# Halving the score steps of the last attention, and a new order of all steps, in a two-layer transformer kernel

## The chip, the cores and the metric

One Trainium2 chip; the program runs on one of its cores. The metric is device time in microseconds (us), the median of the runs shown. A core has a matrix engine (TensorE, PE in the rows; PEld is its weight load), a vector engine (VectorE, DVE), a scalar engine (ScalarE, ACT), GpSimd (POOL) and SyncE (SP), which here only issues transfers. Each engine works through its own list of instructions in order and waits on semaphores that the others raise.

## The reference, cut to what matters

Eight batch elements of 256 tokens by 128 features go through two transformer layers. Layer 0 has a sparse attention, with top-k selected keys, and a two-deep network of window attention and feed-forward parts. Layer 1 has a plain attention with 16 heads of size 8 and a mixture of 16 experts (8 chosen) and a shared one. The change touches only the attention of layer 1:

```python
qkv = x @ W_qkv.T + b_qkv                     # x: (8, 256, 128); 16 heads, head size 8
qkv = qkv.reshape(B, T, H, 3 * hs)
q = qkv[..., :hs]
k = qkv[..., hs:2 * hs]
v = qkv[..., 2 * hs:]
att = jnp.einsum('bthd,bshd->bhts', q, k) / math.sqrt(hs)
att_prob = jax.nn.softmax(att, axis=-1)
att_v = jnp.einsum('bhts,bshd->bthd', att_prob, v)
att_v = att_v.reshape(B, T, C)
return att_v @ W_out.T + b_out
```

All numbers are 32-bit floats.

## The kernel before

**Streams.** The eight batch elements are worked on in four rounds of two. Stream 0 (`s = 0`, memory `arena0`) takes one element of each round and stream 1 (`arena1`) the other; both run everything up to and with the last attention and the layer norm after it. A third stream runs the experts of all eight elements one after the other in the memory `late`. Every stream is a set of Python generators, one for each engine; a `yield` ends a step.

**What sets the order.** `STEPS_IN_TURN` has, for each engine, a string of pairs: a stream, and how many of its steps come next (base 36). So the order on each engine is written out in full, and an instruction can't pass one that stands ahead of it. `IN_ORDER` lists the semaphore signals that each kind of step raises. `BUSY` says how many small filler products (L591, `mean_mat`, results unused) TensorE does at each of 66 places in a round, while it would wait anyway. `LENT` says which bank the experts borrow for each of their results.

**Banks.** The accumulator memory `ps` has 8 banks of 128 rows by 512 floats; stream 0 owns banks 0 to 3 and stream 1 banks 4 to 7. `claim(banks, signals)` says with which signal a bank becomes empty again; in between the expert stream may borrow it.

**The last attention, for one element.** A head takes 16 of 128 rows, 8 of them its features and one a row for the maximum. There are two groups `G` of eight heads, and two halves of the 256 tokens, so four units `v`. In a unit:
- Scores (L1118): eight products. Product `(j, q)` uses rows 32q to 32q+31 and writes half `j` of bank `q`. A product of 32-bit floats is recorded as two MATMUL, so a unit is a row `x16` of the trace and an `x8` of the order.
- Maxima (L2049): VectorE reads banks 0 and 1 in one reduction and banks 2 and 3 in another, then writes the negated maxima (L2055) and raises `x_neg`. The scores of the next unit wait for that `x_neg`, since they write all four banks.
- After four units the maxima are turned (L1127) and added to the queries (L2062).
- Turned scores (L1157): for each unit the same eight products with queries and keys exchanged, again into all four banks. ScalarE takes one exponential for each bank (L1566), raises `st_exp` after each, and the next unit waits for the fourth.
- After units 1 and 3, `values1` (L1137) multiplies the probabilities with the values, into bank 0; ScalarE copies it out (L1260, `x_o`). Then come the sums (L1166), their reciprocal and the output product (L1172).

The stretches that the text calls scores, middle and experts' stretch of a round are: the scores of stream 0; the turned scores of stream 0 with the scores of stream 1; the turned scores of stream 1 with the experts of stream 0's element.

Of the kernel before, what the change touches and what calls it, by code (L numbers as in the profile page):

```python
# [49 lines left out]
def shape_constants():  # L50
# [47 lines left out]
    "pe": ("0912021302110213021204120e1206140317061707130213041305160313011401120212051302110213051308110c130a12011101120612"  # L98
            "02120613021a0317011a05150212021601120416051208110c12051105110216081106110213011202150218041c02150216011102180218"
            "0213021202130113011202110112011202120212041223012102210221021101261123122111210121112312211102211102112112021102"  # L100
            "2102110212031204110111021203210312032712211221021207120422022102210615011703130113012113022312231721160514041205"
            "120811071205110a110211081208120111021202190418031c041502150312021e0512031107120a12051402120811061102110112021702"
            "18041c041a011202180218021302120214011401110212011201120312011204112211012212220223022102110123112212011125112111"
            "0213210221022102112102122212211105120211032112022412031203122112031506172213221307132202210221072103190114011202"
            "22122113051304110512051103110c130a140211061402130617021301170215021a0612011801160112091308120c140a13021108110814"
            "01130217021a0415021502150112021802180213021202130113011202110112011202120112011204112211012212220223022102112202"
            "1123122302112102210221022111021121130521021102120312021301110323120326022512071221041202211202210722031201110112"
            "022117021321132113011902140414051305110312071105120111091102130814061102140115021f021a0415051a0416051208130c1105"
            "1107160811061102130112021502180317011502150217011802180213021202160212011101120312011202120212031122112712211124"
            "1124122111231121132n"),  # L110
# [231 lines left out]
def program(nc, A, out, idx_scratch, score_scratch):  # L342
    ctx = ExitStack()
    with ctx:
# [235 lines left out]
        def tensor_stream(pe, s):  # L580
# [265 lines left out]
            for r in range(ROUNDS):  # L846
# [295 lines left out]
                for v in range(4):  # L1142
                    G, c = v // 2, v % 2
                    if v == 2:
                        yield from values1(0)
                        yield
                        pe.wait_ge(*at("x_o", 1))
# [507 lines left out]
        def vector_stream(dve, st, s):  # L1655
# [147 lines left out]
            for r in range(ROUNDS):  # L1803
# [236 lines left out]
                for v in range(4):  # L2040
# [5 lines left out]
                    for half in range(2):  # L2046
# [3 lines left out]
                        if half == 0:  # L2050
                            yield
# [369 lines left out]
```

## Time and profile before

| | us |
|---|---|
| median of 3 runs | 1385.41 |
| the runs | 1385.41, 1389.0, 1380.8 |
| the profiled execution | 1387.57 |
| its span, first to last instruction | 1385.7 |
| TensorE busy | 1217.4 (88%) |
| VectorE busy | 906.4 (65%) |
| ScalarE busy | 878.2 (63%) |
| GpSimd busy | 364.9 (26%) |

The span is that of the trace; 1.9 us of the profiled execution lie outside it. "Busy" is the time in which at least one instruction ran on the engine, so products that run beside each other count once. TensorE is idle for 168 us, and part of its busy time is filler.

### The profile page before, as it was taken

What the parts mean: (1) busy time and instruction counts of PE and PEld (TensorE: products, weight loads), DVE (VectorE), ACT (ScalarE), POOL (GpSimd) and SP (SyncE); (2) the same over time, 40 slices, a digit from 0 to 9 for tenths busy, and PEclk for the clock granted to TensorE, in tenths of its full rate; (3) what the DMA queues carried; (4) which work ended last, traced back from release to release, by engine and by line L of the source; (5) the groups of instructions that cost most, each with busy time, mean ns of one, the idle gap of its engine ahead of it and who ended that gap; (6) DMA issues with size and microseconds to landing.
All of it is one profiled execution on the core that took longest, in us unless ns stands there. A gap on an engine that the chain in (4) does not pass through costs nothing.

```text
span 1385.7 us, 29670 instructions
## 1 busy us (share of the span) xinstructions
PE 1217.4 (88%) x11271; PEld 847.7 (61%) x11271; DVE 906.4 (65%) x2920; ACT 878.2 (63%) x2243; POOL 364.9 (26%) x580
## 2 busy tenths in 40 slices
PE   7779988789999898888899988887998989889897
PEld 6446655556676665555667755554676656556566
DVE  3966577657475867665766677765667486666533
ACT  3426687646665777755865777764847556874573
POOL 0710232212340423310532143311324042321022
PEclk9889999999999999999999999999999988999998
DMA  8121000000120000000112000000021000000000
GB/s 304 47 79 28 2 1 1 1 5 1 55 75 21 15 2 1 1 1 5 50 24 84 4 6 1 1 1 5 2 74 56 19 17 2 1 0 1 1 1 9
DMA packets 31791, 34.82 MB, mean 25 GB/s; under 512 B 19169, under 2 KB 23713, under 8 KB 31137
## 3 DMA queue, kind: packets, MB, share of 16 engines
q1 hardware_dynamic: 31648, 32.92, 7.9%
q8 instruction: 90, 1.47, 0.4%
q14 instruction: 53, 0.43, 0.1%
HBM read 25.46 MB, written 7.44 MB: 24 GB/s over the span
## 4 chain that ended last, share of the span: by engine, by line
PE 52%; DVE 20%; ACT 18%; issue 4%; DMA 1%; SPq 1%; POOL 1%; DVEq 0%; POOLq 0%; ACTq 0%
PE ps L624 4%; ACT arena L1513 4%; PE ps L1222 3%; ACT arena L1260 3%; DVE small L2049 3%; PE ps L804 3%; PE ps L1232 2%; PE ps L1213 2%; PE ps L687 2%; ACT arena L1566 2%; PE ps L1044 2%; PE ps L746 2%; PE ps L731 2%; PE ps L1118 2%; PE ps L762 2%
## 5 line engine op out<-in xcount | busy, mean ns | idle before, releaser
L1260 ACT ACTIVATE arena<-ps 128x512 f32<-128x512 f32 (+5 forms) x544 | 255.3, 490 | 203.9 <-PE ps L770 29.3
L2231 POOL TENSOR_TENSOR arena<-arena 128x512 f32<-128x512 f32 x64 | 81.9, 1289 | 262.0 <-DVE arena L1722 260.7
L1513 ACT ACTIVATE arena<-arena,small 128x128 f32<-128x128 f32 (+1 forms) x256 | 130.2, 513 | 7.4 <-DVE small L1986 7.2
L1697 DVE CUSTOM_DVE_ANT_0 arena<-ps,mask_w_bf 128x128 f32<-128x128 f32 (+1 forms) x256 | 67.6, 320 | 83.1 <-PE ps L746 82.9
L2049 DVE TENSOR_REDUCE small<-ps 128x4 f32<-128x1024 f32 x64 | 75.4, 1219 | 29.1 <-PE ps L1118 28.8
L1910 DVE TENSOR_TENSOR gath<-ps,rank_tab 96x512 f32<-96x512 f32 x96 | 62.3, 681 | 34.5 <-PE ps L632 22.6
L1566 ACT ACTIVATE arena<-ps 128x512 f32<-128x512 f32 x128 | 66.5, 607 | 26.8 <-PE ps L1157 26.7
L1222 PE MATMUL ps<-w_experts,late 128*128 128x128 f32 x544 | 72.8, 288 | 7.2 <-DVE late L2157 6.7
L1222 PEld LDWEIGHTS ps<-w_experts,late 128*128 128x128 f32 x544 | 68.5, 200 | 15.6 <-DVE late L2157 9.5
L1460 ACT ACTIVATE arena<-arena,small 128x224 f32<-128x224 f32 (+1 forms) x128 | 56.8, 448 | 27.3 <-DVE small L1934 27.1
L2101 DVE SCALAR_TENSOR_TENSOR late<-ps,late 128x128 f32<-128x128 f32 x128 | 39.3, 354 | 52.7 <-PE ps L1222 51.4
L804 PE MATMUL ps<-w_wqkv,arena 128*128 128x512 f32 x128 | 64.2, 637 | 10.4 <-DVE arena L1675 7.7
L1685 DVE TENSOR_TENSOR arena<-arena,small 128x512 f32<-128x512 f32 x96 | 69.9, 728 | 3.1
L591 PE MATMUL ps<-mean_mat 128*128 128x256 bf16 x437 | 62.9, 286 | 9.0 <-ACT arena L1260 4.3
L687 PE MATMUL ps<-packed,arena 128*128 128x128 f32 x384 | 63.2, 289 | 6.6 <-DVE arena L1688 3.6
L1213 PE MATMUL ps<-late,w_experts 128*128 128x256 f32 x256 | 67.2, 401 | 1.8 <-ACT arena L1260 1.7
L1232 PE MATMUL ps<-late,w_experts 128*128 128x256 f32 x256 | 66.8, 395 | 0.8 <-ACT arena L1260 0.7
L687 PEld LDWEIGHTS ps<-packed,arena 128*128 128x128 f32 x384 | 44.6, 146 | 28.9 <-issue 23.9
L2324 POOL TENSOR_TENSOR late<-late 128x256 f32<-128x256 f32 x32 | 23.6, 739 | 145.2 <-ACT late L1634 143.3
L624 PE MATMUL ps<-hot_ring,arena 128*96 128x512 bf16 x192 | 51.3, 407 | 11.6 <-DVE gath L1910 5.7
L591 PEld LDWEIGHTS ps<-mean_mat 128*128 128x128 bf16 x437 | 42.5, 102 | 28.2 <-issue 13.9
L1213 PEld LDWEIGHTS ps<-late,w_experts 128*128 128x128 f32 x256 | 49.4, 199 | 14.0 <-ACT arena L1260 3.6
(296 smaller groups left out, 2980.5 us busy)
## 6 DMA issues: line engine op xcount, KB each, us to landing
idxb<-idx_scratch SPq DMA_DIRECT2D x24, 512.0 KB, 5.2
score_scratch<-arena SPq DMA_DIRECT2D x96, 64.0 KB, 1.7
w_experts<-in_experts SPq DMA_DIRECT2D x3, 1088.0 KB, 16.2
w_wqkv<-in_wqkv SPq DMA_DIRECT2D x1, 1536.0 KB, 9.3
arena<-score_scratch SPq DMA_DIRECT2D x96, 16.0 KB, 2.0
arena<-in_x SPq DMA_DIRECT2D x8, 128.0 KB, 2.1
out_x<-late SPq DMA_DIRECT2D x8, 128.0 KB, 1.9
packed<-in_packed SPq DMA_DIRECT2D x2, 503.0 KB, 4.1
```

The lines of the kernel that those rows point to most:

```text
L591: mm(to, still[:, 0:P], still, start=True, stop=True)
L624: last = mm(bank[g % 2][0:GF, :], m.kv_part[i][:, 0, :], hot[n][:, part], start=(i == 0), stop=(n < 2 and i == 2))
L687: last = pe.transpose(bank[2][:, cols(h)], probs[:, h, :], ident[:, :])
L804: mm(bank[2 * k + j], m.sh[:, cols(k)], wqkv[:, l, 512 * j:512 * j + 512], start=True, stop=True)\
L1213: last = mm(bank[:, L * h:L * h + L], experts[:, 0, 4 * i - 3 + 2 * j + h, :], late.hT, start=True, stop=True)
L1222: last = mm(ups[j][:, L * h + P * k:L * h + P * k + P], late.moe_h[:, first:first + P], experts[:, 2, e, :], start=True, stop=True)
L1232: last = mm(ups[j][:, L * h:L * h + L], experts[:, 1, 4 * i - 3 + 2 * j + h, :], late.hT, start=True, stop=True)
L1260: return act.activation(dst, src, ACT.Copy)
L1513: ins = act.activation(probs, probs, ACT.Exp, bias=nb[s][:, i, h:h + 1], scale=cqs[s][:, T, hh_:hh_ + 1], accum_out=ls[s][:, i, h:h + 1])
L1566: act.activation(m.PT1[v][:, q, :, :].rearrange("p j n -> p (j n)"), bank[q], ACT.Exp, scale=SCALE_1)\
L2049: st.mark(dve.tensor_reduce(to, src, AX.X, ALU.max))
L2231: ins = pool.tensor_tensor(own, own, turned, ALU.add)
```

## The change

The four banks of a unit are handled as two halves: banks 0 and 1 (half 0) and banks 2 and 3 (half 1). A half has four products instead of eight. In the scores, VectorE signals each of its two reductions (`x_max`), and a half waits only for the reduction that read its two banks. In the turned scores, a half waits for the two exponentials that read its banks. For unit 2, half 1 is issued ahead of the value product of units 0 and 1, and half 0 (which shares bank 0 with it) behind; for unit 3, half 1 comes first too. The instructions on VectorE and ScalarE are the same, one to one, but for when they wait; ScalarE has 86 loads of its function tables in place of 88. TensorE has 494 filler products in place of 437. The strings of steps, fillers and banks lent are new from end to end, for all engines.

```diff
 STEPS_IN_TURN = {
-    "pe": ("0912021302110213021204120e1206140317061707130213041305160313011401120212051302110213051308110c130a12011101120612"
+    "pe": ("0912021102120212021204120712071209120812051202120211071203120112011102120213011302130216021305180816071105120511"
...
-    "last_mm": ["x_proj"] * 3 + ["x_mm"] * 4 + ["m_turned"] + ["st_mm"] * 2 + ["x_pv"] + ["st_mm"] * 2 + ["x_pv", "x_sum", "x_out"],
-    "last_act": ["x_q", "x_v"] + ["st_exp"] * 8 + ["x_o"] + ["st_exp"] * 8 + ["x_o", "x_rs"],
-    "last_dve": ["x_k"] + ["x_neg"] * 4 + ["x_aug", "x_on"],
+    "last_mm": ["x_proj"] * 3 + ["x_mm"] * 8 + ["m_turned"] + ["st_mm"] * 5 + ["x_pv"] + ["st_mm"] * 3 + ["x_pv", "x_sum", "x_out"],
+    "last_act": ["x_q", "x_v"] + ["st_exp"] * 10 + ["x_o"] + ["st_exp"] * 6 + ["x_o", "x_rs"],
+    "last_dve": ["x_k"] + ["x_max", "x_max", "x_neg"] * 4 + ["x_aug", "x_on"],
...
-                    claim(range(4), ("x_neg", v + 1))
...
-                        pe.wait_ge(*at("x_neg", v))
-                    pe.wait_ge(*at("x_own", G + 1))
-                    for j in range(2):
-                        for q in range(4):
...
+                    for half in range(2):
+                        yield
+                        claim([2 * half, 2 * half + 1], ("x_max", 2 * v + half + 1))
...
+                        if v > 0:
+                            pe.wait_ge(*at("x_max", 2 * v + half - 1))
+                        if half == 0:
+                            pe.wait_ge(*at("x_own", G + 1))
+                        for j in range(2):
+                            for q in (2 * half, 2 * half + 1):
...
+                def turned_scores(v, half):
                     G, c = v // 2, v % 2
+                    yield
+                    claim([2 * half, 2 * half + 1], ("st_exp", 4 * v + 2 + 2 * (half if v < 2 else 1 - half)))
+                    if v == 0:
+                        if half == 0:
+                            keep_busy(bank[1][:, 0:L])
+                            pe.wait_ge(*at("x_aug", 1))
+                    elif (v, half) == (2, 0):
                         pe.wait_ge(*at("x_o", 1))
+                    elif v == 3:
+                        pe.wait_ge(*at("st_exp", 4 * v - 2 * half))
                     else:
-                        pe.wait_ge(*at("st_exp", 4 * v))
+                        pe.wait_ge(*at("st_exp", 4 * v - 2 + 2 * half))
                     for j in range(2):
-                        for q in range(4):
+                        for q in (2 * half, 2 * half + 1):
...
+                for v in range(2):
+                    for half in range(2):
+                        yield from turned_scores(v, half)
+                yield from turned_scores(2, 1)
+                yield from values1(0)
+                yield from turned_scores(2, 0)
+                for half in (1, 0):
+                    yield from turned_scores(3, half)
                 yield from values1(1)
```

**Place 1: TensorE, scores of stream 0 in the last round.** L1118 (L1119 after) are the scores of stream 0; L1060, L1068 and L1079 (L1059, L1067, L1078 after) are the feed-forward products of stream 1. Before:

```order
L1118 MATMUL ps<-arena0 128x256 x8
L1060 MATMUL ps<-arena1,w_w1 128x256 x2
L1060 MATMUL ps<-arena1,w_w1 85x256
L1068 MATMUL ps<-arena1,w_w1 128x256 x2
L1068 MATMUL ps<-arena1,w_w1 85x256
L1118 MATMUL ps<-arena0 128x256 x8
L1079 MATMUL ps<-arena1,w_w2 128x256 x3
```

After:

```order
L1119 MATMUL ps<-arena0 128x256 x8
L1059 MATMUL ps<-arena1,w_w1 128x256 x2
L1059 MATMUL ps<-arena1,w_w1 85x256
L1119 MATMUL ps<-arena0 128x256 x8
L1067 MATMUL ps<-arena1,w_w1 128x256 x2
L1067 MATMUL ps<-arena1,w_w1 85x256
L1119 MATMUL ps<-arena0 128x256 x8
L1078 MATMUL ps<-arena1,w_w2 128x256 x3
L1119 MATMUL ps<-arena0 128x256 x4
```

Three pairs of halves and the first half of the last unit stand among the feed-forward products of stream 1, where two of the four units stood.

**Place 2: TensorE, the middle of the last round.** L1157 (L1159 after) are the turned scores of stream 0, L1118 (L1119) the scores of stream 1, L1137 the value product. Before:

```order
L1157 MATMUL ps<-arena0 128x256 x8
L1118 MATMUL ps<-arena1 128x256 x8
L1137 MATMUL ps<-arena0 32x256 x16
L1157 MATMUL ps<-arena0 128x256 x8
L1118 MATMUL ps<-arena1 128x256 x8
L1157 MATMUL ps<-arena0 128x256 x8
L1118 MATMUL ps<-arena1 128x256 x8
L1137 MATMUL ps<-arena0 32x256 x16
L1118 MATMUL ps<-arena1 128x256 x8
```

After:

```order
L1159 MATMUL ps<-arena0 128x256 x8
L1119 MATMUL ps<-arena1 128x256 x8
L1159 MATMUL ps<-arena0 128x256 x8
L1119 MATMUL ps<-arena1 128x256 x8
L1159 MATMUL ps<-arena0 128x256 x4
L1137 MATMUL ps<-arena0 32x256 x16
L1119 MATMUL ps<-arena1 128x256 x4
L1159 MATMUL ps<-arena0 128x256 x8
L1119 MATMUL ps<-arena1 128x256 x8
L1159 MATMUL ps<-arena0 128x256 x4
L1119 MATMUL ps<-arena1 128x256 x4
L1137 MATMUL ps<-arena0 32x256 x16
```

The same work stands in ten runs of scores in place of eight (one of the eight stands ahead of the rows shown), four of them single halves, and one half stands ahead of the first value product.

**Place 3: ScalarE, the last round, where the exponentials of stream 1 meet the experts.** L1566 (L1575 after) are the exponentials, L1611 and L1620 (L1617, L1626) the SiLU of the experts, ACT_TABLE_LOAD a load of a function table, L1634 (L1640) the weighting of two experts. Before:

```order
L1566 ACTIVATE arena1<-ps 128x512 x4
L1600 ACTIVATE late<-ps 128x32
L1604 ACTIVATE late<-ps 128x256
L1605 ACTIVATE late<-ps 128x128
L1251 ACT_TABLE_LOAD
L1611 ACTIVATE late<-ps 128x256
L1620 ACTIVATE late<-ps 128x512 x2
L1249 ACT_TABLE_LOAD
L1566 ACTIVATE arena1<-ps 128x512 x4
L1251 ACT_TABLE_LOAD
L1620 ACTIVATE late<-ps 128x512 x2
L1260 ACTIVATE arena1<-ps 128x256
```

After:

```order
L1575 ACTIVATE arena1<-ps 128x512 x6
L1275 ACTIVATE arena0<-ps 128x256
L1575 ACTIVATE arena1<-ps 128x512 x2
L1281 ACTIVATE arena0<-ps,eps_col 128x256
L1285 ACTIVATE arena0<-arena0 128x256
L1575 ACTIVATE arena1<-ps 128x512 x2
L1270 ACTIVATE arena1<-ps 128x256
L1606 ACTIVATE late<-ps 128x32
```

Ten of the sixteen exponentials stand ahead of the experts' first instruction where four stood; fewer changes of table are left behind it.

## Rows read from the trace of the kernel before

**Rows 1.** The page: the span, and each engine's busy time with its instructions.

```profile
span 1385.7 us, 29670 instructions
...
PE 1217.4 (88%) x11271; PEld 847.7 (61%) x11271; DVE 906.4 (65%) x2920; ACT 878.2 (63%) x2243; POOL 364.9 (26%) x580
```

**Rows 2.** The page: the chain that ended last, by engine.

```profile
PE 52%; DVE 20%; ACT 18%; issue 4%; DMA 1%; SPq 1%; POOL 1%; DVEq 0%; POOLq 0%; ACTq 0%
```

**Rows 3.** Groups by line: count | busy us, mean ns | idle before, releasers.

```profile
L2049 DVE TENSOR_REDUCE small<-ps 128x4 f32<-128x1024 f32 x64 | 75.4, 1219 | 29.1 <-PE ps L1118 28.8
...
L1566 ACT ACTIVATE arena<-ps 128x512 f32<-128x512 f32 x128 | 66.5, 607 | 26.8 <-PE ps L1157 26.7
...
L591 PE MATMUL ps<-mean_mat 128*128 128x256 bf16 x437 | 62.9, 286 | 9.0 <-ACT arena L1260 4.3 <-ACT arena L1341 3.6 <-DVE arena L1707 1.0
...
L1251 ACT ACT_TABLE_LOAD x43 | 55.2, 1283 | 0.8
...
L1118 PE MATMUL ps<-arena 32*128 32x256 f32 x512 | 38.0, 412 | 13.2 <-DVE arena L2055 11.5 <-POOL arena L2305 1.7
L1157 PE MATMUL ps<-arena 32*128 32x256 f32 x512 | 37.4, 406 | 7.4 <-ACT arena L1566 5.7 <-DVE arena L2062 1.0 <-ACT arena L1260 0.5
```

**Rows 4.** Windows, the four score stretches summed: all work, then L591 alone.

```profile
sum 66.00, PE 55.86 PEld 38.20 DVE 52.54 ACT 19.30 POOL 6.43; mean PE 13.96 PEld 9.55 DVE 13.13 ACT 4.83 POOL 1.61
...
sum 66.00, PE 3.88 PEld 2.73; mean PE 0.97 PEld 0.68
```

**Rows 5.** Windows, the four middle stretches summed: all work, then L591 alone.

```profile
sum 119.00, PE 95.77 PEld 61.15 DVE 67.52 ACT 58.57 POOL 12.92; mean PE 23.94 PEld 15.29 DVE 16.88 ACT 14.64 POOL 3.23
...
sum 119.00, PE 9.17 PEld 6.96; mean PE 2.29 PEld 1.74
```

**Rows 6.** Windows, the four experts' stretches summed: all work.

```profile
sum 161.00, PE 148.16 PEld 106.83 DVE 91.38 ACT 128.25 POOL 41.51; mean PE 37.04 PEld 26.71 DVE 22.84 ACT 32.06 POOL 10.38
```

**Rows 7.** Timeline, TensorE, scores of the last round: start us, us, what.

```profile
1263.59 1.15 PE L1118 MATMUL ps<-arena 32*128 32x256 f32 x16
...
1266.40 1.99 PE L1044 MATMUL ps<-arena,w_wo 128*128 128x256 f32 x8 [0.48 <-ACT arena L1260]
1268.32 1.15 PE L1118 MATMUL ps<-arena 32*128 32x256 f32 x16
...
1270.72 0.70 PE L605 MATMUL ps<-arena,mean_mat 128*128 128x256 f32 x2
1272.15 1.15 PE L1118 MATMUL ps<-arena 32*128 32x256 f32 x16 [0.73 <-DVE arena L2055]
1273.23 1.56 PE L1060 MATMUL ps<-arena,w_w 128*128 128x256 f32 x6
```

**Rows 8.** Chain of waits, third round and (last row) last round: start us, us, what.

```profile
954.64 2.08 ACT arena L1566 x4
...
956.76 1.93 PE ps L1137 x32
...
962.33 0.19 DVE arena L2055
...
962.56 1.19 PE ps L1118 x16
...
963.77 2.37 DVE small L2049 x2
...
1302.76 2.35 DVE small L2049 x2
```

**Rows 9.** Timeline, TensorE, middle of the last round.

```profile
1283.44 1.15 PE L1157 MATMUL ps<-arena 32*128 32x256 f32 x16 [1.02 <-DVE arena L2062]
1284.87 1.99 PE L1098 MATMUL ps<-arena,packed 128*128 128x256 f32 x8 [0.29 <-DVE arena L1668]
...
1293.01 1.15 PE L1157 MATMUL ps<-arena 32*128 32x256 f32 x16 [0.51 <-ACT arena L1260]
1293.98 1.04 PE L1118 MATMUL ps<-arena 32*128 32x256 f32 x16
```

More of the change, by code:

```diff
@@ L1105, in tensor_stream @@
                     G, T = v // 2, v % 2
[L1106 to L1121 removed]
+                    for half in range(2):
+                        yield
+                        claim([2 * half, 2 * half + 1], ("x_max", 2 * v + half + 1))
+                        if (v, half) == (0, 0):
+                            keep_busy(bank[1][:, 0:L])
+                            pe.wait_ge(*at("x_k", 1))
+                            pe.wait_ge(*at("x_v", 1))
+                        if v > 0:
[4 more added lines that the diff above has]
+                            for q in (2 * half, 2 * half + 1):
+                                rows_ = slice(32 * q, 32 * q + 32)
+                                last = mm(bank[q][:, L * j:L * j + L], m.q_own[rows_, G, j, cols(T)], m.k1[rows_, G, :],
+                                          start=True, stop=True)
+                        last.then_inc(*one("x_mm"))
                 yield
@@ L2042, in vector_stream @@
                     yield
+                    for half in range(2):
+                        if half == 1:
+                            yield
+                        dve.wait_ge(*at("x_mm", 2 * v + half + 1))
+                        src = ps[:, 4 * s + 2 * half:4 * s + 2 * half + 2, :].rearrange("p q (j n) -> p q j n", j=2)
+                        to = mx1[s][:, T, 8 * G + 4 * half:8 * G + 4 * half + 4].rearrange("p (q j) -> p q j", j=2)
+                        dve.tensor_reduce(to, src, AX.X, ALU.max).then_inc(*one("x_max"))
+                    yield
                     if v == 0:
                         dve.wait_ge(*at("m_zero", 1))
-                    dve.wait_ge(*at("x_mm", v + 1))
-                    for half in range(2):
-                        src = ps[:, 4 * s + 2 * half:4 * s + 2 * half + 2, :].rearrange("p q (j n) -> p q j n", j=2)
-                        to = mx1[s][:, T, 8 * G + 4 * half:8 * G + 4 * half + 4].rearrange("p (q j) -> p q j", j=2)
-                        st.mark(dve.tensor_reduce(to, src, AX.X, ALU.max))
-                        if half == 0:
-                            yield
-                    yield
-                    st.wait()
+                    dve.wait_ge(*at("x_max", 2 * v + 2))
                     to = m.mneg[:, T, G, :].rearrange("p (h n) -> p h n", n=HR)[:, :, D1]
```

120 lines of the change are left out of this document (48 added, 72 removed).

## The prediction, made before the change was run

> **What bounds the kernel now.** I read the page first. TensorE is busy 88% of the span, the next engine 65% [rows 1], and the chain of waits lies on TensorE for 52% and on VectorE and ScalarE for 38% [rows 2]. So no engine is the bound by itself: TensorE has 168 us of idle time, and where the chain leaves it, something short and serial is under way. Then I looked at the stretches that the change touches. Score and middle stretches together last 185 us; in them TensorE idles 10.1 + 23.2 us and spends 3.9 + 9.2 us on fillers, 46.4 us in all [rows 4, 5]. The experts' stretches, 161 us, have only 12.8 us idle, so TensorE is 92% busy there [rows 6]. The reader is to see two regimes: a middle in which waits for banks set the pace, and a stretch behind it in which TensorE's own work does.
>
> In the middle the wait is a ping-pong between an engine and the banks. For scores: reductions 2.37, negation 0.19, products 1.19, and the little time between, a period of 3.83 (the second L1118 of the pattern runs from 962.56, its reductions from 963.77; 962.33 is the negation before it) [rows 8]. For turned scores: exponentials 2.08 and products 1.19, about 3.33. VectorE has 64 reductions of 1219 ns and ScalarE 128 exponentials of 607 [rows 3], and neither overlaps with the products of its own stream.
>
> **What a half costs TensorE.** This decides the case. A full unit is eight products in four row tiles, two to a tile. One product over the full array, of the same 256 columns, takes 0.70 us, and four take 1.99, so 0.43 more for each. Eight in four tiles take 1.15, which is what two in a row should take (0.70 + 0.43 = 1.13) [rows 7]. So the tiles run beside each other, and the time goes by the products in one tile. A half has four products in two tiles: again two to a tile. My value is that it lasts 1.15 and keeps the engine 1.08, the time from a unit's start to that of the next product of full size (1272.15 to 1273.23) [rows 7]. It does half the work in the time of the whole, since two tiles stand idle. The other end is half the price, 0.54, if the products were limited by how fast they are issued; the 0.43 per product speaks against that. A half that stands right behind the other half, with its wait already over, uses the idle tiles, so such a pair costs one unit. The trace of before has no such pair; I take the tiles as independent because the four of a unit are.
>
> In the new order the 128 halves stand in 85 runs where 64 units stood: 45 single halves, 37 pairs, 3 triples. At least 21 more run times: 21 × 1.08 = 23 us. If no pair overlapped, because its second half still waits, 64 × 1.08 = 69 us.
>
> There is a rule against the change beside this. A unit of row tiles followed by another of row tiles starts it 0.97 later (1293.01 to 1293.98) [rows 9], a product of full size 1.08 later [rows 7]: a change of tiling costs some 0.1. With 21 more runs and a change at either side that is 42 × 0.11 = 4.6 us at most, and it is already in the 1.08. The Trainium skill, TensorEngine Tiling (Array Packing), section Key Properties, says that a change of tiling mode drains TensorE; it gives no price. The trace agrees in sign with its 0.11, and by the rule the sum would be no other.
>
> **The change part by part.**
>
> *Score stretches.* Alone, with halves, VectorE never waits: while it reduces one half, the other is refilled, 1.15 for 1.18. The period falls from 3.83 to 2.37 + 0.19 = 2.56, for three transitions 3.8 us per element. But stream 1's feed-forward lies between. In the last round the stretch takes 1263.59 to 1283.44, 19.9 us [rows 7, 9]. Following the new order (pair, L1059, pair, L1067, pair, L1078, two halves) with the durations above, L1059 (1.56 [rows 7]) and its like ahead of a waiting half and two extra VectorE steps of the feed-forward between, I come to about 16.6. Saved 3.2 at best; I take 2, since each wait met late passes to both streams.
>
> *Middle stretches.* The last round, from the first turned score (t = 0). Unit 0 of stream 0 gives exponentials from 1.2 to 3.3; its unit 1 follows in halves at 2.25 and 3.3, exponentials until 5.6. Half (2,1) must wait for all of unit 1, since its banks come free last: 5.6, exponentials 6.8 to 7.8. The value product (1.93 [rows 8]) runs behind it, 6.4 to 8.3, its copy to 8.8, then (2,0) and (3,1), exponentials 10.0 to 12.1, and (3,0), until 13.3. Stream 1's scores stand between: reductions 2.2 to 4.5, 4.8 to 7.1, then its (2,0), which is held behind the value product until 8.3: 9.5 to 12.1, and 12.3 to 14.7. Before, the same ran from 1283.44 to 1305.11 (1302.76 + 2.35), 21.7 us, of which 2.0 are L1098, now ahead [rows 8, 9]: 19.7. Saved 5.0 on paper, if all is in time. The stretch would hold 8 units' work in 10 runs and at least two pairs whose second half waits. I take 3.5.
>
> *Experts' stretches.* Stream 1's turned scores are 8 halves for 4 units. In the last round 6 runs, elsewhere similar: 2.2 us more if all pairs overlap, 4.3 if none does. TensorE is 92% busy, so it is paid; I take 3. The shorter wait of ScalarE gains nothing there, since the experts filled it.
>
> *Table loads.* 88 to 86; the two that go stand in the last round, where the exponentials of stream 1 go ahead of the experts (place 3). ScalarE is on the chain there, 1.28 each [rows 3]: −2.6. The other end is 0.
>
> *Fillers.* 57 more of 62.9/437 = 0.144 us [rows 3]: 8.2 us if none was covered. 36 of the 57 stand in the first eight places of the two streams, while weights load; the rest where a wait is due. I take +1; below nothing is possible too, if they keep the clock up.
>
> *All other steps.* They are the same instructions in a new order, over the 1040 us outside the stretches, with 168 − 10.1 − 23.2 − 12.8 = 122 us of TensorE idle [rows 1, 4 to 6]. I see no term in it and take 0, with ±8 (some 2 us a round either way, the size of one wait moved).
>
> Sum: 4 × (−2 − 3.5 + 3) − 2.6 + 1 = −11.6. On the profiled execution, 1387.6, that is 1376.0; that execution lies 2.2 above the median of the runs shown, 1385.4, so the same on the median is 1373.8. I predict 1375.
>
> **The rivals.**
>
> *A, the chain gives all of it (faster still).* Pairs overlap whenever they stand together, and the walks above come true: 4 × (−3.2 − 5.0 + 2.2) − 2.6 = −26.6, about 1359. For it: 33.3 us of plain idle in the two kinds of stretch. Against: stream 1's halves are held behind stream 0's waits on one in-order engine. Chance 0.20.
>
> *B, given back (no change).* Stream 1 gets its scores sooner but its turned scores meet the dense experts' stretch, and TensorE pays 4.3 there, 2 more in the scores and middle each: 4 × (−5.5 + 4 + 4.3) would be +11; with half of the extra work in time that was idle, about 0: 1386. For it: 92%. Chance 0.25.
>
> *C, TensorE becomes the bound (slower).* No half overlaps another: 69 us of new TensorE time. It decides once this exceeds what the stretches have to give: 46.4 idle and filler, of which some 16 can't be used, since dense windows too keep 8% idle. So 69 − 30 = 39 more, less the 22 of waits saved: +17, 1402. For it: half (1,1) waits for a reduction 1.18 behind that of (1,0), longer than the 1.08 the first keeps the engine. Against: where feed-forward products stand ahead of the pair, both waits are over. Chance 0.15.
>
> *D, the new order outside loses (slower).* A transfer or an expert's bank comes due later; +8 on no gain, 1394. Nothing in the profile speaks for it but the size of the move. Chance 0.07.
>
> My forecast has 0.33, its own range 1366 to 1384. That the change does nothing at all is excluded by the order.
>
> **How the numbers follow.** Within 0.5% (about 7 us) of 1385.4 is what a measurement can't tell from no change: 1378.5 to 1392.3. Faster: A 0.20, the forecast 0.28, B 0.04: 0.52. Same: the forecast 0.05, B 0.19, D 0.02: 0.26. Slower: C 0.15, D 0.05, B 0.02: 0.22. The range 1355 to 1396 leaves out most of C and the lower edge of A, some 0.2.
>
> **What would show it.** L1119 should be recorded in runs of 8 that last 1.15, not 0.6, and TensorE's busy time should rise by 15 to 45 us. Of a pair that wasn't waiting, all 16 records should fit in 1.15 to 1.4. VectorE's idle time before its reductions (29.1) and ScalarE's before the exponentials (26.8) [rows 3] should fall by half. The middle of the last round should take 15 to 17 us. I am wrong if a half lasts 0.6 (then A or better), if TensorE's idle time outside the stretches has moved by more than 10, or if the experts' stretches grew by more than 5 each.

## The result, and the profile after

The changed kernel takes 1395.41 us (median of 17 runs, 1386.25 to 1401.99) against 1384.25 us (17 runs, 1375.12 to 1389.34) for the kernel before in the same comparison: 1.0082 of it, 95% interval 1.0064 to 1.0099. It is 0.8% slower; 1375, faster, had been predicted, in a range of 1355 to 1396 whose upper end belonged to the rivals. Three executions of other kernels (two with the third stretch new, one with the pairs put together), more than 1.5% above the fastest of their kernel at a lower clock, are left out of the ratios and means below. The page of the profiled execution, answering to [rows 1] and, in its last line, to [rows 2]:

```profile
span 1393.2 us, 29754 instructions
...
PE 1240.4 (89%) x11328; PEld 867.4 (62%) x11328; DVE 901.7 (65%) x2920; ACT 877.4 (63%) x2241; POOL 365.8 (26%) x580
...
PE 51%; ACT 18%; DVE 17%; issue 4%; POOL 3%; DMA 2%; SPq 1%; POOLq 0%; DVEq 0%; ACTq 0%
```

TensorE is busy 23.0 us more and idle 15.5 us less (152.8 for 168.3), and the span grew by 7.5. GpSimd and the transfers hold more of the chain than they did. The groups that answer to [rows 3]:

```profile
L2055 DVE TENSOR_REDUCE small<-ps 128x4 f32<-128x1024 f32 x64 | 76.8, 1220 | 19.2 <-PE ps L1119 19.1
...
L1575 ACT ACTIVATE arena<-ps 128x512 f32<-128x512 f32 x128 | 67.6, 599 | 23.6 <-PE ps L1159 23.6
...
L590 PE MATMUL ps<-mean_mat 128*128 128x256 bf16 x494 | 77.6, 289 | 5.4 <-ACT arena L1351 2.4 <-ACT arena L1270 1.8 <-DVE arena L1713 1.2
...
L1119 PE MATMUL ps<-arena 32*128 32x256 f32 x512 | 56.4, 398 | 6.5 <-DVE small L2055 4.5 <-POOL arena L2311 1.1 <-issue 0.7
L1159 PE MATMUL ps<-arena 32*128 32x256 f32 x512 | 54.7, 399 | 5.7 <-ACT arena L1575 3.0 <-DVE arena L2068 1.6 <-ACT late L1626 0.2
```

The idle time before the reductions fell from 29.1 to 19.2 and that before the exponentials from 26.8 to 23.6. The two groups of scores take 111.1 us of TensorE for 75.4, the fillers (the small products with unused results) 77.6 for 62.9. The timeline of TensorE over the last round's scores and the beginning of its middle (start us, us, what), beside [rows 7, 9]:

```profile
1278.27 1.16 PE L1119 MATMUL ps<-arena 32*128 32x256 f32 x16 [0.30 <-POOL arena L2311]
1279.39 1.56 PE L1059 MATMUL ps<-arena,w_w 128*128 128x256 f32 x6
1280.88 2.09 PE L1119 MATMUL ps<-arena 32*128 32x256 f32 x16
1282.91 1.56 PE L1067 MATMUL ps<-arena,w_w 128*128 128x256 f32 x6
1284.40 1.21 PE L1119 MATMUL ps<-arena 32*128 32x256 f32 x16
1285.54 1.56 PE L1078 MATMUL ps<-arena,w_w 128*128 128x256 f32 x6
1287.03 1.13 PE L1119 MATMUL ps<-arena 32*128 32x256 f32 x8
...
1296.10 1.16 PE L1159 MATMUL ps<-arena 32*128 32x256 f32 x16
1297.07 1.15 PE L1119 MATMUL ps<-arena 32*128 32x256 f32 x16
...
1301.72 1.13 PE L1159 MATMUL ps<-arena 32*128 32x256 f32 x8
1302.78 1.93 PE L1137 MATMUL ps<-arena 128*32 128x256 f32 x32
...
1312.72 1.13 PE L1176 MATMUL ps<-arena,packed 128*128 128x512 f32 x2
```

A single half (`x8`) lasts 1.13 and the two halves of an unwaiting pair together (`x16`) 1.16; where the second half waits, the pair lasts up to 2.09. The scores of this round go from 1278.27 to 1296.10, 17.8 us (19.9 before), and the middle to the sums at 1312.72, 16.6 us. Before, the sums came 19.2 us after the first turned score, but 2.0 of these were stream 1's L1098, whose counterpart L1097 now stands in the scores' stretch.

So the place that was changed did get shorter. Where the time went shows in windows over everything else, from the end of stream 1's last attention to the beginning of stream 0's next (and from the start of the program to the first): first all work, then the fillers alone; of the kernel before,

```profile
sum 982.00, PE 871.69 PEld 601.66 DVE 668.27 ACT 645.78 POOL 288.82; mean PE 217.92 PEld 150.42 DVE 167.07 ACT 161.44 POOL 72.21
...
sum 982.00, PE 46.62 PEld 30.46; mean PE 11.66 PEld 7.61
```

and of the one after:

```profile
686.00:934.00 248.00, 221.84 (x2130) 154.09 (x2128) 168.64 (x571) 171.21 (x461) 81.33 (x130) 0.97 0.08 23
1012.00:1275.00 263.00, 234.51 (x2216) 165.00 (x2216) 172.45 (x579) 179.76 (x474) 85.99 (x136) 0.95 0.08 23
sum 1013.50, PE 895.14 PEld 622.91 DVE 677.95 ACT 663.72 POOL 308.26; mean PE 223.79 PEld 155.73 DVE 169.49 ACT 165.93 POOL 77.07
...
sum 1013.50, PE 65.93 PEld 41.07; mean PE 16.48 PEld 10.27
```

Outside the last attentions the kernel is 31.5 us longer: 19.3 of fillers, 8.1 of idle time (118.4 for 110.3) and 4.1 of other TensorE work. The last attentions are 24.0 us shorter (403.7 to 379.7). The difference, 7.5, is the span's.

Not all of the 24.0 is a gain, and not all of the 31.5 a loss: work has moved from the one to the other. The same windows hold 17.9 us more of ScalarE's work (645.78 to 663.72) and 19.4 more of GpSimd's (288.82 to 308.26), while the whole kernel has no more of either (878.2 and 877.4, 364.9 and 365.8). The fillers in them are 421 for 313, of 57 more in all. What the halves alone are worth is read from the first experiment.

### The profile page after: what moved, and what is told of

Its sections match the earlier page's. It is cut to its first block, busy times and chain, and to the rows that moved or that the text cites. A ratio compares the mean times of both kernels' runs of the same rounds, so it can differ in the third digit from the quotient of the medians.

```text
span 1393.2 us, 29754 instructions
## 1 busy us (share of the span) xinstructions
PE 1240.4 (89%) x11328; PEld 867.4 (62%) x11328; DVE 901.7 (65%) x2920; ACT 877.4 (63%) x2241; POOL 365.8 (26%) x580
## 4 chain that ended last, share of the span: by engine, by line
PE 51%; ACT 18%; DVE 17%; issue 4%; POOL 3%; DMA 2%; SPq 1%; POOLq 0%; DVEq 0%; ACTq 0%
ACT arena L1523 4%; ACT arena L1270 4%; PE ps L623 3%; PE ps L1159 3%; PE ps L1232 3%; PE ps L1119 3%; PE ps L803 3%; PE ps L1223 3%; PE ps L1242 2%; PE ps L1137 2%; PE ps L686 2%; DVE arena L1703 2%; DMA idxb<-idx_scratch 2%; PE ps L745 2%; ACT arena L1575 2%
## 5 line engine op out<-in xcount | busy, mean ns | idle before, releaser
L1270 ACT ACTIVATE arena<-ps 128x512 f32<-128x512 f32 (+6 forms) x544 | 254.9, 489 | 213.3 <-PE ps L769 30.4
L2055 DVE TENSOR_REDUCE small<-ps 128x4 f32<-128x1024 f32 x64 | 76.8, 1220 | 19.2 <-PE ps L1119 19.1
L1575 ACT ACTIVATE arena<-ps 128x512 f32<-128x512 f32 x128 | 67.6, 599 | 23.6 <-PE ps L1159 23.6
L590 PE MATMUL ps<-mean_mat 128*128 128x256 bf16 x494 | 77.6, 289 | 5.4 <-ACT arena L1351 2.4
L1916 DVE TENSOR_TENSOR gath<-ps,rank_tab 96x512 f32<-96x512 f32 x96 | 62.5, 681 | 27.7 <-PE ps L623 13.7
L686 PE MATMUL ps<-packed,arena 128*128 128x128 f32 x384 | 62.3, 286 | 15.3 <-DVE arena L1698 4.8
L590 PEld LDWEIGHTS ps<-mean_mat 128*128 128x128 bf16 x494 | 47.6, 103 | 30.9 <-issue 17.6
L2163 DVE TENSOR_TENSOR late<-late,ps 128x512 f32<-128x512 f32 x64 | 43.3, 684 | 32.4 <-PE ps L1242 27.3
L803 PE MATMUL ps<-w_wqkv,arena 128*128 128x512 f32 x128 | 61.4, 614 | 1.7 <-DVE arena L1681 1.6
L1119 PE MATMUL ps<-arena 32*128 32x256 f32 x512 | 56.4, 398 | 6.5 <-DVE small L2055 4.5
L745 PE MATMUL ps<-arena 64*128 64x192 f32 (+1 forms) x512 | 56.9, 345 | 5.4 <-DVE small L1992 3.9
```

Of the source, the lines that this page charges most:

```text
L590: mm(to, still[:, 0:P], still, start=True, stop=True)
L686: last = pe.transpose(bank[2][:, cols(h)], probs[:, h, :], ident[:, :])
L745: last = mm(bank[j][:, n * i:n * i + n], m.qT[rows_, 2 * half + i, cols(T)], m.kT[rows_, 2 * half + i, key_cols(T)], start=True, stop=True)
L803: mm(bank[2 * k + j], m.sh[:, cols(k)], wqkv[:, l, 512 * j:512 * j + 512], start=True, stop=True)\
L1119: last = mm(bank[q][:, L * j:L * j + L], m.q_own[rows_, G, j, cols(T)], m.k1[rows_, G, :], start=True, stop=True)
L1270: return act.activation(dst, src, ACT.Copy)
```

## The experiments

All ratios are to the kernel before on the same chip, with 95% intervals. "Old order" is the kernel before with its own strings, fillers and lent banks; "in place" means that the two halves of a unit stand where the unit stood. The diffs are cut to the lines that matter.

**Halves alone, in the old order**

```diff
-                    claim(range(4), ("x_neg", v + 1))
+                    for half in range(2):
+                        claim([2 * half, 2 * half + 1], ("x_max", 2 * v + half + 1))
```

(The turned scores likewise. The strings stay; half (2,1) stays behind the value product.)

> The kernel before, with its strings of steps, its fillers and its lent banks untouched; only each unit of the last attention is written, waited for and freed in two halves, both halves in the step where the unit stood. Theory N (the new order outside the last attention costs, the halving gains): the halving keeps what the changed kernel's trace shows in the last attention, some 10 to 20 us, so 1365 to 1375 and a ratio of 0.987 to 0.993. Theory H (the halving itself costs, since a half keeps TensorE 1.13 us as a whole unit does, and other streams wait behind it): 1389 to 1397, ratio 1.003 to 1.009, as the changed kernel.

Measured 1373.79, ratio 0.9928 [0.9901, 0.9955]. Its groups of reductions and exponentials:

```profile
L2055 DVE TENSOR_REDUCE small<-ps 128x4 f32<-128x1024 f32 x64 | 75.3, 1216 | 17.7 <-PE ps L1120 17.6
...
L1572 ACT ACTIVATE arena<-ps 128x512 f32<-128x512 f32 x128 | 66.5, 606 | 19.2 <-PE ps L1161 19.1
```

Both waits shrink more than in the changed kernel (29.1 and 26.8 to 17.7 and 19.2). By the traces stream 0's time from its first scores to its sums, over the four rounds, fell from 160.6 to 152.1 us, which is about the gain. The halves are a gain of 0.7%; what turns it into a loss of 0.8% is the rest of the change.

**Scores alone, turned scores alone**

```diff
-                    claim(range(4), ("x_neg", v + 1))
+                        claim([2 * half, 2 * half + 1], ("x_max", 2 * v + half + 1))
```

in the first, and in the second only its counterpart:

```diff
-                    claim(range(4), ("st_exp", 4 * v + 4))
+                    claim([2 * half, 2 * half + 1], ("st_exp", 4 * v + 2 + 2 * half))
```

> As halves_in_old_order, but only the scores with the maxima (L1118, L2049) are halved; the turned scores stay whole. Theory N: VectorE's ping-pong is the longer one (3.83 against 2.56 us a unit), so over half of the gain of both, ratio 0.992 to 0.997. Theory H: in the scores most second halves must wait for a reduction and keep TensorE blocked, so this part carries the loss, ratio 1.002 to 1.006.

> As halves_in_old_order, but only the turned scores with the exponentials (L1157, L1566) are halved. Theory N: a quarter to a half of the gain of both, ratio 0.995 to 0.999. Theory H: half of its turned scores stand among the experts, where TensorE is 92% busy, so it loses there, ratio 1.001 to 1.005.

Measured 0.9948 [0.9931, 0.9965] and 1.0005 [0.9984, 1.0027]. The gain lies in the scores, whose banks VectorE reads. In the profiled executions the turned halves by themselves shorten the middle stretches by 1.8 us in all and lengthen the experts' stretches by 2.4; both are of the size by which these stretches differ from one kernel to another.

**The same instructions, but no early release**

```diff
+HALVED_X, HALVED_T = (), ()         # each half is signalled, the wait is for the whole unit
```

> The kernel before with the signals of the halves (x_max after each reduction, one signal for each half unit) but with every unit still issued whole and every wait for the whole unit, in the old order. If the 0.7% of halves_in_old_order come from the early release of the banks, this is the kernel before: 0.998 to 1.002. If they come from something beside it (other semaphores, code positions), it is as fast as halves_in_old_order, 0.991 to 0.996.

Measured 1.0013 [0.9982, 1.0044]; the reductions wait as before:

```profile
L2087 DVE TENSOR_REDUCE small<-ps 128x4 f32<-128x1024 f32 x64 | 75.4, 1218 | 28.2 <-PE ps L1121 27.9
```

28.2 stands against 17.7, and the gain is gone with it. It is the release by halves that gains, not the finer signals.

**Turned scores of one stream**

```diff
+HALVED_X, HALVED_T = (), (0,)       # the second run (1,)
```

> Old order; only the turned scores of stream 0, which stand in the middle stretches, are halved. The prediction's two regimes (gain where waits set the pace, loss where TensorE or ScalarE is dense) say: faster than halve_turned_only (1.0005), 0.996 to 0.999. If there are no such regimes: about half of nothing, 0.999 to 1.002.

> Old order; only the turned scores of stream 1, which stand among the experts, are halved. Two regimes: slower than the kernel before, 1.001 to 1.004. No regimes: 0.999 to 1.002.

Measured 1.0028 [1.0002, 1.0053] and 0.9984 [0.9963, 1.0005]. Both small, and in the direction opposite to what was expected: stream 1, among the dense experts, doesn't pay for its halves. The prediction's "two regimes" find no support here.

**One half ahead of the value product, in the old order**

```diff
+                        turned_half(2, 1)
                         values1(0)
-                        turned_half(2, 1)
                         turned_half(2, 0)
```

> halves_in_old_order, and half (2,1) of the turned scores moved ahead of the value product of units 0 and 1, with its two exponentials ahead of the copy out of bank 0, as the changed kernel has it; half 1 comes first in unit 3 too. The rest of the order is the old one. Theory N: the move is worth the 1 us for each element that two exponentials last, where ScalarE is waited for; 3 to 8 us under halves_in_old_order, ratio 0.987 to 0.991. Theory S: the lone half adds 1.08 us of TensorE each time, 8 in all, and eats it: 0.992 to 0.996.

Measured 0.9986 [0.9961, 1.0011], so 0.58% (8 us) slower than with both halves behind. ScalarE's copy of the value product now stands behind two more exponentials and the value product behind one more half (1.13), eight times in the kernel. The middle stretches, 76.5 us in all with both halves behind, are 82.9 with one ahead, and the experts' stretches 183.4 for 179.5; that the copy and the value product are the whole of it was not shown by itself.

**The new order with the old fillers; with the pairs put together**

```diff
-BUSY = [... of the changed kernel ...]
+BUSY = [... of the kernel before ...]
```

> The changed kernel with the table of fillers of the kernel before (437 small products, at the same 66 places of a round, in place of 494; their busy time grew from 62.9 to 77.6 us). Theory F (the fillers cost): it wins back 5 to 10 us, ratio to the kernel before 1.001 to 1.005. Theory N and H, in which the fillers run in idle time: within 3 us of the changed kernel, ratio 1.006 to 1.010.

```diff
+MERGED = {("x", 0, 0, 1): "E", ...}  # 24 of the 27 scattered pairs: both halves at one place
```

> The changed kernel, whose order leaves 27 pairs of halves of one unit apart (besides those of unit 2, which the value product parts). In 24 of them both halves now stand at one place, 23 at that of the first half and one at that of the second; every half still waits for its own banks alone, and nothing else moves. Theory S (the scattered halves cost: L1119 and L1159 keep TensorE busy 106.8 us here against 85.6 with the halves paired in the old order, and the difference is the loss): TensorE's score time falls by 10 to 20 us and the time by as much, so a ratio to the kernel before of 0.995 to 1.001. Theory N (the new order of everything else costs): the score time falls, the time stays within 4 us of the changed kernel, 1.005 to 1.011.

Measured 1.0307 [1.0279, 1.0334] and 1.0297 [1.0253, 1.034]. Neither mends anything. But the second run doesn't test what it was made for: the scores' time on TensorE was to fall by 10 to 20 us and is 108.5 for 106.8 (in the old order with all halves 85.6). In 23 of the 24 pairs the second half was drawn forward to the first, where it can hold up the queue until its banks are free. So it shows that joining the halves in this way costs 2% more; whether scattered halves cost something in the changed kernel stays open. In both kernels the mean granted clock of the profiled execution is 0.949, against 0.970 in the changed kernel:

```profile
core 0: 1430.9 us, clock 0.949
```

**No fillers at all: in the kernel before, and in the changed kernel**

```diff
-BUSY = [("b0h303...
+BUSY = [("000000...
```

> The kernel before without any filler product (L591, 437 of them, 62.9 us busy). new_order_old_fillers was 30 us slower than the changed kernel with fewer fillers at other places, and its granted clock fell from 0.97 to 0.949. Theory F (the fillers are worth what they keep up of TensorE's clock): the clock falls below 0.95 and the time rises by over 2%. The rival, that fillers are paid as work: the time falls.

> The changed kernel without any filler product. If its loss against the kernel before is one of the order, it is behind old_order_no_fillers by 0.5 to 2% as well. If the loss lies in its 57 additional fillers, or in where they stand, it is level with it or ahead.

Measured 1.0107 [1.0057, 1.0158] and 1.0212 [1.0171, 1.0252]. So all fillers together are worth 1.1% in the kernel before and 1.3% in the changed one: they don't cause the loss. Without any of them the changed kernel is still 1.04% slower, halves included.

**The two orders mixed.** Both orders pass through (nearly) the same state, the same number of steps taken by every stream on every engine, each time stream 0 begins a round. So the strings, fillers and lent banks can be cut there and joined. All of these kernels have the changed kernel's halves.

(The next two diffs are schematic: one word for each stretch or part, in place of the strings themselves.)

```diff
-STEPS_IN_TURN, BUSY, LENT = new, new, new, new
+STEPS_IN_TURN, BUSY, LENT = old, old, new, old   # third_round_new
```

> Both orders are cut at the three places where stream 0 begins a new round; there both have taken the same steps on every engine, but for 2 to 6. Each of the four stretches of steps, with its fillers and lent banks, can so come from the old order or from the new one. The halves are the changed kernel's everywhere. Old in all four is the old order with half (2,1) ahead, 0.9986 of the kernel before; new in all four is the changed kernel, 1.0082. Here the third stretch alone is new (old, old, new, old). Theory L, the loss lies in the stretch itself: in the traces the third round is 335.9 us long in the changed kernel and 325.0 in the old order with the half ahead, so +10.9 us or 0.8%: 1.006, and the round is 333 to 338 long. Rival W, the loss is spread or is handed on from earlier stretches: a quarter of 0.96%, 1.001. Rival J, orders that were made whole lose wherever they are joined: 1.008 or more.

> The counterpart: new, new, old, new. Theory L: the changed kernel less 10.9 us, 1.0082 - 0.0079 = 1.000, the third round 323 to 327 us long. Rival W: 1.0082 - 0.0024 = 1.006. Rival J: 1.01 or more.

> Old, new, old, new. By the starts of stream 0's rounds in the traces the new order loses 5.7 us in the first stretch, gains nothing or 0.5 in the second, loses 10.9 in the third and gains 0.4 in the fourth. Theory L: level with the old order throughout, 0.998 to 0.999. Rival W: half of the loss, 1.003. Rival J: 1.01 or more.

> Old, new, new, new. Theory L: the changed kernel less the 5.7 us of the first stretch, 1.004, with the third round still 333 to 338 us long. Rival W: 1.006; the two are near each other here, and the length of the first round tells (312 against 317 us for the start of stream 0's second round). Rival J: 1.01.

| stretches | ratio | third round of stream 0, us |
|---|---|---|
| old old old old (the half ahead; not cut) | 0.9986 [0.9961, 1.0011] | 324.9 |
| old old **new** old | 1.0085 [1.0052, 1.0117] | 334.8 |
| new new old new | 1.0124 [1.0090, 1.0158] | 331.9 |
| old new old new | 1.0158 [1.0121, 1.0195] | 328.4 |
| old new new new | 1.0160 [1.0115, 1.0205] | 334.9 |
| new new new new (the changed kernel; not cut) | 1.0082 [1.0064, 1.0099] | 335.8 |

With the third stretch alone new the kernel is as slow as the changed one, and the round has the length that theory L gave it (333 to 338). But L had 1.006 for the kernel and J 1.008 or more, so the ratio of 1.0085 fits J better. The converse fails: taking the third stretch out again, or the first, makes the kernel slower still, as rival J had it. One reason shows at the joins. In the changed kernel stream 0's first products of the round (L855) stand ahead of stream 1's last scores (L1119),

```profile
645.43 0.38 PE L855 MATMUL ps<-packed,arena 128*128 128x128 f32 x2
645.74 1.16 PE L1119 MATMUL ps<-arena 32*128 32x256 f32 x16
```

and in third_round_old the cut has put them (L813 there) behind (L1077, L1085):

```profile
642.63 1.38 PE L1077 MATMUL ps<-arena 32*128 32x256 f32 x16
645.82 1.13 PE L1077 MATMUL ps<-arena 32*128 32x256 f32 x8 [1.81 <-DVE small L2013]
648.49 1.11 PE L1085 MATMUL ps<-packed,arena 128*128 128x128 f32 x4 [1.54 <-DVE arena L2019]
649.40 0.64 PE L813 MATMUL ps<-packed,arena 128*128 128x128 f32 x2
```

From stream 0's sums to its next round it is 15.3 us there and 8.4 in the changed kernel: three or four steps, moved by the cut, come with 7 us. It is the cut and not the change of order that does this: in first_round_old both sides of this join are new, and it is 13.1 us. The join in third_round_new moved nothing of this (7.6 us, as in the old order), so it is the cleaner one; the one at the end of its third stretch is 9.5 for 7.9. No run cuts the old order and joins it again unchanged, so how much of these ratios the joins cost is not known.

Where the round gets longer the traces tell without any join, in the changed kernel itself (each is one execution). In microseconds of stream 0's third round:

| kernel | start to first scores | first scores to sums | sums to next round |
|---|---|---|---|
| old order, half ahead | 276.2 | 40.9 | 7.9 |
| changed kernel | 291.8 | 35.5 | 8.5 |
| third stretch new | 289.9 | 35.5 | 9.5 |

Stream 0 loses 13.7 to 15.6 us on its way to the last attention and wins 5.4 back in it. Over all four rounds of the changed kernel it is 28.2 us lost on the way and 13.2 won in the attentions. So the loss lies outside the last attention, and over half of it in the third round. It can be placed more closely by the output products of stream 0's two window layers. From the first to the second it is 56.2, 64.7, 56.5 and 60.4 us in the four rounds of the old order with the half ahead, and 66.6, 61.7, 74.7 and 67.1 in the changed kernel; with the third stretch alone new it is 73.1 in that round. This distance takes up the whole loss.

**Inside the third stretch.** Both orders meet twice more in it: in stream 0's gather, and in its second window layer.

```diff
-third stretch = new, new, new
+third stretch = old, old, new     # third_round_last_part_new; the other has old, new, new
```

> Within the third stretch both orders pass through the same state twice more, with no step moved by a cut there: in stream 0's gather (some 60 us into the round) and in its second window layer, once its first queries and keys are turned (some 225 us in). Here only the part behind the second cut is new, until the next round begins; all else is old with the half ahead (0.9986; with the whole third stretch new 1.0085). In the trace of the latter stream 0 has its second f_o 14.9 us later in the round than in the old order, its first 1.7 earlier, stream 1 its first 7.6 later. Theory E, the delay is made ahead of the cut and handed down: 1.000 at most (+2 us), the round 325 to 328 long. Theory Z, it is made behind the cut, where stream 0's second window layer and stream 1's first stand behind each other: 1.006, the round 332 to 336 long.

> The same with the middle part new too, so that only the front of the round (to the gather) is old. Theory E with the front as the cause (its q2 products come 6.2 us later in the round): 1.000. Theory E with the middle as the cause: 1.006 to 1.008. Theory Z: 1.006, as with the last part alone.

Measured 1.0110 [1.0074, 1.0147] and 1.0136 [1.0089, 1.0183]. By these times, the last part alone, some 100 us of the program with a window layer and stream 0's last attention in it, is enough for the loss, as theory Z had it; but Z wanted a round of 332 to 336 us, and with the last part new it is 329.4 (338.8 with both). The timeline of the four output products of window layers (each stream's two) in this round, old order with the half ahead:

```profile
833.01 1.99 PE L1044 MATMUL ps<-arena,w_wo 128*128 128x256 f32 x8
...
858.86 1.89 PE L1044 MATMUL ps<-arena,w_wo 128*128 128x256 f32 x8
...
889.50 1.99 PE L1044 MATMUL ps<-arena,w_wo 128*128 128x256 f32 x8 [0.48 <-ACT arena L1275]
...
922.30 1.99 PE L1044 MATMUL ps<-arena,w_wo 128*128 128x256 f32 x8 [0.48 <-ACT arena L1275]
```

and with the last part new:

```profile
838.21 1.99 PE L1001 MATMUL ps<-arena,w_wo 128*128 128x256 f32 x8
...
864.06 1.89 PE L1001 MATMUL ps<-arena,w_wo 128*128 128x256 f32 x8
...
900.08 1.99 PE L1001 MATMUL ps<-arena,w_wo 128*128 128x256 f32 x8
...
929.42 1.99 PE L1001 MATMUL ps<-arena,w_wo 128*128 128x256 f32 x8
```

The third of them, stream 0's second, comes 61.9 us after its first instead of 56.5, and the next 29.3 behind it instead of 32.8. On TensorE the new order has put nine more steps of stream 1 (174 in place of 165 since the cut) ahead of it. So stream 0 gives way to stream 1 here. It doesn't lose its next round by it, though: from the second product shown to stream 0's next round it is 105.6 us with the last part new and 105.3 in the old order, since the last attention is 5.4 shorter. Of the 4.5 us by which the round is longer, 4.2 are there before that second product, among steps that are in the old order in both kernels. And 8.4 more lie in the last round, again of the old order in both, at a mean granted clock of 0.947 for 0.979. So that this last part makes the kernel slow by holding stream 0 back is not borne out by the trace, and why this kernel is slow stays open; a join and a lower clock are the rivals left. Nor does the last part make most of the distance between stream 0's two products: 56.5 us in the old order, it is 61.9 with the last part new, 71.6 with the last two parts and 73.1 with the whole stretch.

**The best guess**: halves in the old order, in place, but turned scores whole in stream 1.

```diff
+HALVED_X, HALVED_T = (0, 1), (0,)
```

> Old order; the scores of both streams and the turned scores of stream 0 are halved, those of stream 1 are not. Two regimes: faster than halves_in_old_order (0.9928) and halve_scores_only (0.9948), 0.988 to 0.992. No regimes: level with them.

Measured 1372.13 against 1382.41, 0.9919 [0.9894, 0.9943]: level with all halves in the old order, and like it faster than both kernels.

**What the clock has to do with it.** Each execution has a span and a mean granted clock. In 165 executions of the 19 kernels other than the one before, taken as deviations from the mean of their own kernel, 0.01 less clock goes with 6.3 us more (correlation −0.72). The means can so be put to one clock, 0.967:

| kernel | mean span | mean clock | span at 0.967 |
|---|---|---|---|
| kernel before (103 executions) | 1381.5 | 0.9642 | 1379.7 |
| halves in the old order | 1371.0 | 0.9708 | 1373.4 |
| the same, one half ahead | 1380.7 | 0.9700 | 1382.6 |
| last part of the third stretch new | 1396.5 | 0.9605 | 1392.4 |
| third stretch new | 1393.6 | 0.9654 | 1392.5 |
| changed kernel | 1393.2 | 0.9676 | 1393.6 |
| kernel before, no fillers | 1396.2 | 0.9495 | 1385.1 |
| changed kernel, no fillers | 1411.3 | 0.9475 | 1398.9 |
| new order, old fillers | 1424.4 | 0.9552 | 1416.9 |
| new order, pairs put together | 1424.9 | 0.9558 | 1417.8 |

This is a correlation used as a correction, not a cause that was shown. The half ahead costs 9.2 us by it and the whole new order 11.0 on top. Two thirds of what the fillers are worth goes with the clock. It doesn't explain the last two rows: at one clock they are still 23 to 24 us above the changed kernel, and what costs these was not found.

## Why the prediction was wrong

**The step that failed** is "All other steps. They are the same instructions in a new order, over the 1040 us outside the stretches ... I see no term in it and take 0, with ±8." The runs show a loss in its place. With the halves, the old order and the half ahead the kernel is at 0.9986, and with the new order at 1.0082: +1.0%, or +11.0 us at one clock, of the whole order, what it gains inside the attentions already taken off. On stream 0's way to its last attentions alone it is 28.2 us in the traces, far beyond the bound of 8. Rival D had the mechanism, "the new order outside loses", with a chance of 0.07 and the remark that nothing spoke for it "but the size of the move". The loss lies between stream 0's two window layers. The cause that D gave, a transfer or an expert's bank that comes due later, was not tested, and which moved steps make the loss stays open. The prediction looked at three places of the order and treated all others as noise around nothing. In the runs it had only one side: each of the six kernels in which the two orders were cut and joined was slower than the kernel before (1.0085 to 1.0160). Its own sign for this, "TensorE's idle time outside the stretches has moved by more than 10", would have missed it: 8.1 us are idle time, and 19.3 are fillers.

The other steps:

- **A half costs TensorE 1.15, a pair one unit**: right (1.13 and 1.16). Scores take 32.4 us more of TensorE (as the time in which at least one of them runs, 74.4 to 106.8), inside 23 to 69. TensorE's busy time rose by 23.0, inside 15 to 45, the additional fillers included.
- **Score stretches −2 a round**: by the starts of stream 0's scores and turned scores, 77.5 to 71.4 us in all, −1.5 a round; with the halves alone, in the old order, 75.5, −0.5 a round. The walk of the last round (16.6) came out 17.8.
- **Middle stretches −3.5 a round**: 83.2 to 73.9 us, −2.3 a round; with the halves alone 76.5, −1.7 a round. The last round's 15 to 17 came out 16.6. But half (2,1) ahead of the value product, which the walk counted as a gain, is a loss of 0.58% by its own run. Halved scores alone bring the middle stretches to 80.3 and halved turned scores alone to 81.4.
- **Experts' stretches +3 a round**: wrong. From stream 0's sums to stream 1's, 179.7 us fell to 173.1, −1.6 a round, with other streams' work moved out; with the halves alone they stay at 179.5, and halving stream 1's turned scores costs nothing (0.9984). So the extra TensorE time of the halves went into gaps, in stretches that are 92% busy too.
- **Waits to fall by half**: those before the reductions fell by a third, those before the exponentials by an eighth. In the old order it was 39% and 28%.
- **Table loads −2.6**: two loads fewer, of 1.28 each; whether they were on the path no run tells.
- **Fillers +1**: 14.7 us more of them are recorded, against 8.2 us at most; without any filler the changed kernel is 1.3% slower. Their number is no cost by itself; "if they keep the clock up" was named and not priced.

Taken together, the windows of the attentions shrank by more than the sum had (24.0 us, moved work included, against 12.6 with the table loads), and the rest of the program took 31.5.

For the halves alone the sum has 4 × (−2 − 3.5 + 3) = −10.0, and −9.0 was measured (1382.74 to 1373.79). That this is near is luck in part: by the trace the three terms are −0.5, −1.7 and 0.0 a round, so gains that were put too high stood against a cost that isn't there.

## What to carry to other kernels

Change the mechanism first inside the old order, and time that; a new order made along with it is a second change, and here it was the dearer one: −0.7% for the halves, +0.6% for one half moved ahead, +1.0% for the rest of the order. Release a buffer in the pieces in which its reader reads it, where the reader has idle time before it; the extra cost of small instructions on the busiest engine was hidden here in its gaps. And when a whole order is replaced, follow in both traces the stream that starts the next round, stretch by stretch: here it lost 28 us on its way to the last attentions, and won back 13 in them. An order that is cut and joined is a third order; run the cut without the exchange as well.

## What the runs showed of the hardware

- Four products of 32 rows in two of the four row tiles take 1.13 us, as long as eight in all four (1.15). Two such groups in different tiles, one behind the other, take 1.16 together: the tiles run beside each other across groups too.
- The granted clock falls without the fillers, and slower executions have a lower clock. Mean clock over the executions: 0.9642 before and 0.9495 without fillers; 0.9676 in the changed kernel, 0.9475 without them, and 0.9552 with the old order's 437 fillers in the new order. Small products that compute nothing are worth 1.1 to 1.3% here, and 437 of them at places made for another order are worse than none (1.0307 against 1.0212), though the clock is higher with them than without.
